# Eleven expert passes of 75 slots instead of twelve of 76, all x batches on chip, paired items routed 14 points apart, batch 2 prepared 5 points later

## What is computed

```python
def ffn(h):                       # h: (8*512, 256), E = 2, FF = 1024
    probs = softmax(h @ gate_w.T)
    sel, top_w = argmax(probs), max(probs)
    y = (silu(h @ w_gate[e].T) * (h @ w_up[e].T)) @ w_down[e].T     # for each expert e
    return y[sel] * top_w
x = x + 0.5 * ffn(layernorm(x))
x = x + attn(layernorm(x))        # attn(v): rms_norm, q/k/v, causal softmax, Wo, plus v itself
x = x + 0.5 * ffn(layernorm(x))
```

## Time and profile before

| | |
|---|---|
| median of 3 runs | 1248.18 us (1243.98 to 1249.4) |
| the profiled execution | 1243.21 us, span 1241.5 us |
| PE, DVE, ACT, POOL busy | 88%, 70%, 60%, 46% of the span |
| mean granted PE clock | 0.955 |

### The profile page before, as it was taken

One profiled execution on the slowest core, in us unless ns is written; L12 is line 12 of the kernel. 1 busy time (PEld: TensorE's weight loads), 2 busy tenths in 40 slices (PEclk: granted clock), 3 DMA queues, 4 the chain that ended last, 5 costly groups with the idle time before them and its releaser, 6 DMA issues. The chain is left out here.

```text
span 1241.5 us, 38522 instructions
## 1 busy us (share of the span) xinstructions
PE 1086.5 (88%) x14214; PEld 930.8 (75%) x14214; DVE 867.9 (70%) x1790; ACT 747.7 (60%) x1289; POOL 574.6 (46%) x693
## 2 busy tenths in 40 slices
PE   2787889987989989889988799998999999899894
PEld 1676778866878877778877678876877878788784
DVE  6743647695667886877788868877777788875431
ACT  3532526665657866666676566776666777675321
POOL 3447554254543354645255535334473254655443
PEclk9789899998989999999999899999999999999998
DMA  8103241213121122122122151011321112211112
GB/s 319 64 28 86 74 104 47 69 45 88 57 61 33 35 75 68 39 73 85 51 80 74 41 109 54 28 45 58 84 79 45 46 43 69 79 51 49 53 44 48
DMA packets 108508, 83.30 MB, mean 67 GB/s; under 512 B 57072, under 2 KB 102384, under 8 KB 108336
## 3 DMA queue, kind: packets, MB, share of 16 engines
q1 hardware_dynamic: 90864, 53.56, 15.9%
q0 software_dynamic: 6528, 17.31, 4.5%
q10 hardware_dynamic: 10944, 9.97, 2.4%
HBM read 37.26 MB, written 34.23 MB: 58 GB/s over the span
## 5 line engine op out<-in xcount | busy, mean ns | idle before, releaser
L711 POOL TENSOR_TENSOR h_lo<-hid,h_hi 128x256 bf16<-128x256 f32 x304 | 221.2, 748 | 464.9 <-ACT h_hi L783 461.0
L854 ACT ACTIVATE area<-ps_w,s_scale 128x512 f32<-128x512 f32 x320 | 219.6, 686 | 214.6 <-PE ps_w L1124 90.5
L1077 DVE TENSOR_TENSOR area<-area 128x512 f16<-128x512 f32 x256 | 212.3, 830 | 18.5 <-ACT area L855 16.8
L1221 PE MATMUL ps_g<-x_t,w 128*128 128x128 f16 x1096 | 208.8, 225 | 10.6 <-DVE w L922 5.3
L855 ACT ACTIVATE area<-ps_w,s_scale 128x512 f16<-128x512 f32 x320 | 218.0, 681 | 0.0
L1221 PE MATMUL ps_u<-x_t,w 128*128 128x128 f16 x1096 | 210.3, 225 | 2.3 <-issue 2.1
L1223 PE MATMUL ps_u<-x_t,w 128*128 128x128 f16 x1096 | 210.2, 224 | 2.3 <-issue 2.3
L1223 PE MATMUL ps_g<-x_t,w 128*128 128x128 f16 x1096 | 209.1, 225 | 1.3 <-issue 1.3
L1222 PE MATMUL ps_u<-x_t,w 128*128 128x128 f16 x1096 | 209.0, 223 | 0.4 <-issue 0.4
L1222 PE MATMUL ps_g<-x_t,w 128*128 128x128 f16 x1096 | 208.1, 224 | 0.2 <-issue 0.2
L1242 PE MATMUL ps_y<-wd,h_hi 128*128 (+1 forms) x608 | 170.1, 280 | 14.4 <-POOL h_lo L711 9.8
(11 more groups left out here) (180 smaller groups left out, 2717.8 us busy)
## 6 DMA issues: line engine op xcount, KB each, us to landing
y_sorted<-ys ACTq DMA_DIRECT2D x76, 128.0 KB
qk_scratch<-area SPq DMA_DIRECT2D x32, 256.0 KB
qt<-qk_scratch SPq DMA_DIRECT2D x128, 64.0 KB, 2.7
kt<-qk_scratch SPq DMA_DIRECT2D x128, 64.0 KB, 2.7
x_buf<-x SPq DMA_DIRECT2D x8, 512.0 KB, 4.3
out<-x_buf SPq DMA_DIRECT2D x7, 512.0 KB, 2.9
x_sorted<-zeros SPq DMA_DIRECT2D x18, 136.0 KB, 4.2
area<-w_down SPq DMA_DIRECT2D x4, 512.0 KB, 13.2
```

The source lines that it names most:

```text
L711: pool.tensor_tensor(h_lo[:, u % 2, c], hid[:, u % 2, c], h_hi[:, u % 2, c], ALU.subtract).then_inc(h_lo_done, 1)
L854: act.activation(p_f32[:, f % 3], ps[:], ACT.Exp, scale=s_scale[:])
L1077: dve.tensor_tensor(p_lo[:, f % 4], p_f32[:, f % 3], p_hi[:, f % 4], ALU.subtract).then_inc(lo_done, 1)
L1221: pe.matmul(cols, w_hi, x_hi, start=kb == 0 and f == 0, stop=False, skip_group_check=True)
```

## The change

Items 6 and 7 of the first layer become one pass, as do items 0 and 1 of the second, and item 2 of the second stands alone: 11 passes, 75 slots, five pairs instead of four. `PASS_AT`, `PART_POINTS` (20.5), `PAIR_LAG` (14), `UPDATE_LAG` (14.5) and the lag of a second item's gather and update (7) change; batch 2 gets a list of its own for its norm (-35 instead of -40 from its first part) and projections. `XBUFS` becomes 8, so that no batch waits for another's buffer. For the room, `ys` and `yt` become single buffers (with waits to fit), and the zeros that clear `x_sorted` at the start lie in the last x buffer. The diff:

```diff
--- before.py
+++ after.py
@@ -63,8 +63,8 @@
 
 
 
-PASSES = [[("first", 0)], [("first", 1)], [("first", 2), ("first", 3)], [("first", 4), ("first", 5)], [("second", 0)],
-          [("second", 1)], [("first", 6)], [("first", 7), ("second", 2)], [("second", 3), ("second", 4)],
+PASSES = [[("first", 0)], [("first", 1)], [("first", 2), ("first", 3)], [("first", 4), ("first", 5)],
+          [("first", 6), ("first", 7)], [("second", 0), ("second", 1)], [("second", 2)], [("second", 3), ("second", 4)],
           [("second", 5)], [("second", 6)], [("second", 7)]]
 ITEMS = [(n, i, what, b) for n, batches in enumerate(PASSES) for i, (what, b) in enumerate(batches)]
 ITEM_OF = {(what, b): k for k, (n, i, what, b) in enumerate(ITEMS)}
@@ -78,7 +78,7 @@
 MAX_SLOTS = max(SLOTS)
 PLACES = MAX_SLOTS * P
 MAX_COUNT = 2**10
-XBUFS = 6
+XBUFS = 8
 ROUTES = 4
 ONES_UNIT = 8
 
@@ -111,15 +111,17 @@
 
 UNIT_POINTS = 6
 SLOT_POINTS = 2 * UNIT_POINTS
-PASS_AT = [SLOT_POINTS * at for at in SLOT_AT[:4]] + [336, 396, 462, 522, 630, 738, 798, 865]
+PASS_AT = [SLOT_POINTS * at for at in SLOT_AT[:6]] + [552, 612, 720, 780, 848]
 PART_AT = 115
-PART_POINTS = 21
+PART_POINTS = 20.5
 FILL_POINTS = PART_POINTS / 10
 LEAD = 33
-PAIR_LAG = 9
+PAIR_LAG = 14
 
 NORM_AT = [-40, -39.5, -38.5, -36, -34, -32.4]
-RESIDUAL_AT = -33
+
+NORM2_AT = [-35, -34.5, -33.5, -31.6, -30.4, -29.3]
+PROJ2_AT = [-28, -26, -24, -22, -20, -18]
 PROJ_AT = [-30.7, -28.2, -25.7, -23.2, -20.7, -18.2]
 STORE_LAG = 1.0
 QK_IN_AT = [-22, -16, -14, -14]
@@ -133,7 +135,8 @@
 EXP_LAG = 0.0
 COEF_LAG = 1.0
 GATHER_LAG = 8
-UPDATE_LAG = 16
+UPDATE_LAG = 14.5
+ITEM_LAG = 7
 OUT_AT = [122, 123.5, 125.5, 127.5]
 ROUTE_STEPS = [("l_stats", 0, 0.0), ("l_stats", 1, 0.5), ("l_rstd", 0, 1.5), ("l_norm", 0, 4.0),
                ("l_split", 0, 6.0), ("l_dlogit", 0, 6.0), ("l_low", 0, 8.5), ("l_exp", 0, 10.5), ("l_prefix", 0, 11.0),
@@ -178,11 +181,11 @@
             put(p + 12.3, "y_store", u // 2)
 
     for k, (n, i, what, b) in enumerate(ITEMS):
-        end = PASS_AT[n] + SLOT_POINTS * SLOTS[n] + 5.2 * i
+        end = PASS_AT[n] + SLOT_POINTS * SLOTS[n] + ITEM_LAG * i
         put(end + GATHER_LAG, "y_gather", k)
         at = end + UPDATE_LAG
         if what == "first":
-            at = min(at, part_at(GROUPS * b, NORM_AT[0]) - 1)
+            at = min(at, part_at(GROUPS * b, (NORM2_AT if b == 2 else NORM_AT)[0]) - 1)
         put(at, "x_update", k)
         at = PASS_AT[n] - LEAD - PAIR_LAG * (len(PASSES[n]) - 1 - i)
         if what == "second":
@@ -210,12 +213,13 @@
         first = GROUPS * b
         norm = [("stats", b, 0), ("stats", b, 1), ("rstd", b), ("norm", b), ("transpose", b, "attn", 0),
                 ("transpose", b, "attn", 1)]
-        for where, stage in zip(NORM_AT, norm):
+        norm_at, proj_at = (NORM2_AT, PROJ2_AT) if b == 2 else (NORM_AT, PROJ_AT)
+        for where, stage in zip(norm_at, norm):
             put(part_at(first, where), *stage)
-        put(part_at(first, RESIDUAL_AT), "residual", b)
+        put(part_at(first, norm_at[3] + 3), "residual", b)
         for m in range(NP):
-            put(part_at(first, PROJ_AT[m]), "proj", b, m)
-            put(part_at(first, PROJ_AT[m] + STORE_LAG), "qk_store", b, m)
+            put(part_at(first, proj_at[m]), "proj", b, m)
+            put(part_at(first, proj_at[m] + STORE_LAG), "qk_store", b, m)
         out = [("transpose", b, "o", 0), ("transpose", b, "o", 1), ("out_proj", b, 0), ("out_proj", b, 1)]
         for where, stage in zip(OUT_AT, out):
             put(part_at(first, where), *stage)
@@ -276,9 +280,9 @@
         xs = xs_rows[:, :, 0:D].bitcast(F16).rearrange("p i (a d) -> p i a d", a=2)
         xs_coef = xs_rows[:, :, D:D + 1]
         x_t = [sb(f"x_t{n}", [P, 2 * KB * PLACES], F16) for n in range(2)]
-        ys = [sb(f"ys{n}", [P, D], F32) for n in range(2)]
-        yt = [sb(f"yt{n}", [P, T, D], F32) for n in range(2)]
-        zeros = sb("zeros", [P, XW], F32)
+        ys = sb("ys", [P, D], F32)
+        yt = sb("yt", [P, T, D], F32)
+        zeros = x_buf[XBUFS - 1][:].rearrange("p i d -> p (i d)")[:, 0:XW]
 
         xt_hi = sb("xt_hi", [P, KB, S], F32R)
         xt_lo = sb("xt_lo", [P, KB, S], F32R)
@@ -372,8 +376,8 @@
 
 
         perm = x_t[1][:, 0:T * P * SLOTS[0]].rearrange("p (i t) -> p i t", i=T)
-        places_i = yt[0][:].rearrange("p i d -> p (i d)")[:, 0:P * SLOTS[0]].bitcast(I32)
-        places = yt[1][:].rearrange("p i d -> p (i d)")[:, 0:P * SLOTS[0] // 2].bitcast(F16)
+        places_i = yt[:].rearrange("p i d -> p (i d)")[:, 0:P * SLOTS[0]].bitcast(I32)
+        places = yt[:].rearrange("p i d -> p (i d)")[:, P * SLOTS[0]:P * SLOTS[0] * 3 // 2].bitcast(F16)
         perm_banks = [ps_g, ps_u, ps_v[0], ps_v[1]]
 
         w_in = sems("w_in", PIECES)
@@ -511,7 +515,7 @@
 
             def zero(n, blocks):
                 for i in blocks:
-                    sp.dma_start(x_sorted[n][i * P:(i + 1) * P, :], zeros[:]).then_inc(zeroed[n], 16)
+                    sp.dma_start(x_sorted[n][i * P:(i + 1) * P, :], zeros).then_inc(zeroed[n], 16)
 
             for w in range(PIECES):
                 sp.dma_start(stage[w], raw[w]).then_inc(w_in[w], 16)
@@ -528,6 +532,9 @@
                         sp.wait_ge(x_out[b - XBUFS], 16)
                     elif b >= 3:
                         sp.wait_ge(w_ready, PIECES)
+                    if b == XBUFS - 1:
+                        for n in range(2):
+                            sp.wait_ge(zeroed[n], 16 * MAX_SLOTS)
                     sp.dma_start(x_of(b)[:], batch_view(x, b)).then_inc(x_in[b], 16)
                 elif what == "l_load":
                     n = st[1]
@@ -594,7 +601,7 @@
         @block.gpsimd
         def _(pool):
             link = Links(pool, pool_link)
-            pool.memset(zeros[:], 0.0).then_inc(zero_ready, 1)
+            pool.memset(zeros, 0.0).then_inc(zero_ready, 1)
             pool.memset(xs_rows[:, :, D:], 0.0)
             link(pool.memset(ident[:], 0.0))
             link(pool.affine_select(out=ident[:], in_=ident[:], compare_op=ALU.not_equal, fill=1.0,
@@ -654,7 +661,7 @@
                     n = st[1]
                     b = ITEMS[n][3]
                     pool.wait_ge(gathered[n % 2], 64 * (n // 2 + 1))
-                    pool.tensor_tensor(x_of(b)[:], yt[n % 2][:], x_of(b)[:], ALU.add).then_inc(x_updated, 1)
+                    pool.tensor_tensor(x_of(b)[:], yt[:], x_of(b)[:], ALU.add).then_inc(x_updated, 1)
                 elif what == "coef":
                     n = st[1]
                     pool.wait_ge(coef_loaded[n % 2], 16 * (n // 2 + 1))
@@ -669,8 +676,8 @@
                     p = ITEMS[n][0]
                     for parity in range(2):
                         pool.wait_ge(y_saved[parity], y_stores(p, parity))
-                    if n >= 2:
-                        pool.wait_ge(x_updated, n - 1)
+                    if n:
+                        pool.wait_ge(x_updated, n)
                     if n == len(ITEMS) - 1:
 
                         b = ITEMS[n][3]
@@ -682,7 +689,7 @@
                         continue
                     for i in range(T):
                         pool.indirect_dma_start(
-                            yt[n % 2][:, i, :], None, y_sorted[p % 2][0:P * SLOTS[p], :],
+                            yt[:, i, :], None, y_sorted[p % 2][0:P * SLOTS[p], :],
                             bass.IndirectOffsetOnAxis(ap=place[n % ROUTES][:, i:i + 1], axis=0)
                         ).then_inc(gathered[n % 2], 16)
                 elif what == "rstd":
@@ -784,11 +791,11 @@
                 elif what == "y_out":
                     g = st[1]
                     act.wait_ge(down_done, 2 * g + 2)
-                    if g >= 2:
-                        act.wait_ge(y_saved[g % 2], 16 * (g // 2))
+                    if g:
+                        act.wait_ge(y_saved[(g - 1) % 2], 16 * ((g + 1) // 2))
                     n, s, _ = UNITS[2 * g]
                     act.wait_ge(coef_done, n + 1)
-                    act.activation(ys[g % 2][:], ps_y[:, 0:D], ACT.Copy, scale=coef[n % 2][:, s:s + 1]).then_inc(y_copied, 1)
+                    act.activation(ys[:], ps_y[:, 0:D], ACT.Copy, scale=coef[n % 2][:, s:s + 1]).then_inc(y_copied, 1)
                 elif what == "y_store":
                     g = st[1]
                     n, s, _ = UNITS[2 * g]
@@ -796,7 +803,7 @@
                     if s == 0 and n >= 2:
                         for parity in range(min(ITEM_AT[n - 1], 2)):
                             act.wait_ge(gathered[parity], 64 * ((ITEM_AT[n - 1] + 1 - parity) // 2))
-                    act.dma_start(y_sorted[n % 2][s * P:(s + 1) * P, :], ys[g % 2][:]).then_inc(y_saved[g % 2], 16)
+                    act.dma_start(y_sorted[n % 2][s * P:(s + 1) * P, :], ys[:]).then_inc(y_saved[g % 2], 16)
                 elif what == "norm":
                     b = st[1]
                     act.wait_ge(rstd_done, b + 1)
```

## The result

The changed kernel took 1239.08 us, median of 6 runs (1235.60 to 1242.88), and the kernel before, on the same chip at the same time, 1247.26 us (6 runs, 1243.29 to 1251.87): a ratio of 0.9931, 95% interval 0.9911 to 0.9952, 8 us instead of the 20 forecast. Measured again in a later session it came to 0.9844 (0.9822 to 0.9866), 20 us, and in a third to 0.9956 (0.9928 to 0.9983). So there are two questions: what the change does, and why it does it by different amounts. The second is taken up with the experiments.

A forecast was written before the change was run, and what follows sets the result against it. Good stretches were taken as bound by PE's own work, bad ones by stops of PE. Terms -1.7 - 12.6 - 5 + 3 - 5 + 1.5 + 1 = -18.8 us gave 1227 us, range 1210 to 1246.

The forecast's parts named there:

- All 12.6 us go: In the pairs' preparation, PE's gaps put down to ACT's wait for the scatter, 12.6 us together, vanish with lag 14.
- part 3: Batch 2 prepared later: PE's stop at its stats goes, norm waits behind gather 3; net -5 us (-8 to 0).
- Slot and tail: One slot less: PE's work -5.3 us, +3.6 back as waiting for x_t at the last pass; net -1.7 us.
- Pairs apart: Items of a pair 14 points apart: -12.6 us of PE gaps and -5 us (0 to -10) of clock.
- l_rstd behind the scatter: On POOL in the pairs, l_rstd follows the first item's scatter, so ACT waits: +3 us (0 to +8).
- 3.5 points, 4.4 us: In the pairs, the time from the first item's scatter start to the second's l_norm, giving ACT 1.7 us of wait.
- costs PE up to 2.5: At batch 2's norm, ACT waits 2.3 us or more for rstd behind gather 3, costing PE up to 2.5 us.
- Buffers: Single ys covered, 0; single yt makes POOL wait 1 us once or twice; with queueing +1.5 us (0 to +7).
- Head: Pass 2's first item's l_norm and l_split come before batch 0's norm on ACT: +1 us (0 to +3).
- A: Rival, chance 0.13: POOL's scatter, then l_rstd, stops ACT as long as the landing did; 1245 us.
- B: Rival, chance 0.08: update and gather block POOL 7.3 us at each pair's end, PE waits 5.9 us; 1265 us.
- C: Rival, chance 0.12: the lag does not act as planned, other stops fill the four gaps; 1241 to 1243 us.

The follow-up runs named there:

- xs2: Kernel before with a second xs_rows buffer, so a pair's second l_split no longer waits for the first item's scatter; single ys for room: 0.9946 (0.9930 to 0.9962).
- after_again: The changed kernel itself, unedited, measured again in a later session: 0.9844 (0.9822 to 0.9866) of the kernel before.
- before_again: The kernel before, unedited, run and profiled once more in a later session: 1.0001 (0.9980 to 1.0023).
- session A: The first measuring session: kernel before 1247.26 us, changed kernel 0.9931; PE's stops without a wait 19.3 us before, 20.8 changed.
- lag14: Kernel before with PAIR_LAG 14 instead of 9 in three of its four pairs: 0.9937 (0.9911 to 0.9963).
- after_lag9: Changed kernel with PAIR_LAG back at 9: 0.9961 (0.9941 to 0.9981) of the kernel before.
- after_norm1: Changed kernel without batch 2's own list for norm and projections: 0.9828 (0.9802 to 0.9854) of the kernel before.
- single: Kernel before with only single ys and yt and the lags that go with them: 0.9977 (0.9959 to 0.9995).
- session E: A later measuring session: kernel before 1248.98 us, changed kernel unedited 0.9956; PE's stops without a wait 26.5 us (changed).

## Why the prediction was right and wrong

**The step that failed** is "All 12.6 us go", with -5 of clock behind it: the five gaps that begin while pairs are prepared were put down to ACT's wait for the scatter. xs2, which takes away that wait and leaves the plan alone, won 6.7 us, not 17.6. In its trace, of the 12.6 us the 5.18 of one gap and some 2 of two others went; 2.41 stood unchanged, 2.36 were replaced. The second failure is part 3, -5 booked and 0 measured. Against them stands a gain with no term in the sum: PE's waits for row minima are 19 us shorter in after_again than in before_again, and 13 us shorter in session A.

**Slot and tail (-1.7): right.** PE's work fell by 5.5 us for 5.3 booked, and the idle time in the last routing grew by 3.6 for 3.6. The wait for x_t itself is 1.75 us where 3 to 4 was said; the rest of that idle time is ahead of it.

**Pairs apart (-12.6, clock -5): mechanism right, size wrong for the kernel it was read from.** All of ACT's wait went, but xs2 and lag14 put its worth there at 7 to 8 us. Inside the changed kernel, with five pairs, whose ACT waits would be 28.2 us (after_lag9) and not 20.6, the same edit is worth 14 to 16.

**l_rstd behind the scatter (+3): absent.** In session A the pairs' second items don't wait; in after_again three of five do, 1.1 to 1.5 us each. What failed is "3.5 points, 4.4 us": it goes by the mean of 1.26 us a point, and there a point took 1.8 us.

**Batch 2 (-5): wrong.** 0 within 2 us by after_norm1 and after_again. The failed step is "costs PE up to 2.5": rstd lay behind an h_lo as well as the gather, and PE waited 5.14 us.

**Buffers (+1.5, 0 to +7): too high**, -0.5 to -5 us by single's interval, though single also has the new order of update and gather. The rule of the Trainium skill that was weighed there (Trainium Kernel Development and Optimization, Best Practices: double-buffer so that transfers overlap compute) doesn't bind here, where copies come four landings apart. **Head (+1): a little too small**: PE's wait there grew by 2.2 us, 2.9 between before_again and after_again, because an l_norm that waits 9 us now stands ahead of the batch's norm. I had called that PE's own waiting time, and it was prolonged.

**The mix (0, 5 to either side): the worst-founded term.** The runs at 20.25, 20.75 and 21 points show that it moves the time by 4 to 20 us, tail apart. That after_again met -18.8 by 1 us is therefore partly luck: -14 to -16 from the lag and some -5 from all else, where -14.6 had been reckoned for the one with its clock and its new wait, and -4.2 for the rest, with terms inside both that were wrong.

**The forecast against its first measurement.** The 12 us missed in session A go with the stops without a wait, by the sessions' table; why they come in some sessions stays open. They were in the trace of before, too (19.3 us over its PE rows), and I had not summed them. Had I done so, they would still have stood in both kernels, and I would have written 0.

**The rivals.** A would have needed the wait for l_shift in the pairs, and B long waits for POOL at every pair. One p_lo in session A makes PE wait 5.33 us, near B's 5.9, but one only. C, that other stops fill the four gaps (-4.2 us), is half of what happened in session A and in xs2: two of the gaps did stay or were filled.

## What to carry to other kernels

A stop of the bounding engine is not worth its length. Removing 20 us of ACT's waits gave 7, where PE's gaps beside them, 12.6 us, and the clock had promised 17.6; removing 10.9 us of waits for p_lo gave 25, half clock included. Before gaps are added up, show for each that the wait in question made it: a gap that only stands nearby stays. When a change re-times two interleaved streams, don't book the mix at zero: run the neighbours of the chosen step first, since a quarter of a point was worth more here than any named part but the pairs. And move a reader off a late producer only if something else is moved with it; otherwise the wait takes another name.

## What the runs showed of the hardware

The same program differed between sessions by 29 us (1215.69 and 1244.41 us, the changed kernel) and by 15 us (1233.67 and 1248.98, the one before). Sessions A and E show 19 to 27 us of stops of PE in which it waits for nothing that the trace records, 0.2 to 4.2 us each, near rows of four indirect DMAs on POOL; spreading those DMAs cut them from 26.5 to 11.6 us in session E. What PE lacks in them isn't shown: for the changed kernel each DMA queue's share of the engines' time is the same to 0.3 points in sessions A, C and E. Between session A and the sessions without them, the kernel before shows 21 us less of other waits beside them and the changed one 4 us less; that the stops hide the others is a reading, not a test. In session E VectorE's p_lo took 823 ns while POOL made a fifth of them and 766 ns when POOL made none; what slows it isn't shown.
